# Gated attention and quantised MLP block on one core: means subtracted on GpSimd, MLP weights rounded on VectorE, and four pairs of roots taken together

## What is computed

```python
def _layernorm(x, axis=-1, eps=1e-05):
    return (x - mean(x)) / sqrt(var(x) + eps)

# xattn: q = layernorm(x), k = v = ctx
qp, kp = proj(q), proj(ctx)                  # two 128x128 linears, the same for both
attn   = softmax(qp @ kp.T * 128**-0.5 + mask)
x      = x + tanh(g_xattn) * (attn @ ctx)

# ffn on layernorm(x): fixed_quant(v, 8 bits, f) = clip(round(v * 2**f), -128, 127) / 2**f
h = relu(fixed_quant(fixed_quant(xn, 4) @ fixed_quant(w1, 6).T + fixed_quant(b1, 6), 4))
x = x + tanh(g_ffn) * (fixed_quant(h, 4) @ fixed_quant(w2, 6).T + fixed_quant(b2, 6))
```

## Time and profile before

| | |
|---|---|
| median of 3 runs | 66.66 us (66.5 to 66.83) |
| the profiled execution, its own time | 66.68 us |
| span of that execution, first to last instruction | 64.9 us |
| busy: TensorE, VectorE, ScalarE, GpSimd | 57.8, 54.7, 52.4, 44.5 us |
| granted TensorE clock, mean over the span | 1.0 of full speed |
| last VectorE instruction (the last `result`) | 62.23 to 62.71 us |

### The profile page before, as it was taken

How to read it: one execution, slowest core, us unless ns; L and a number is a source line. 1 busy time by engine, 2 the same in 40 slices (tenths; PEclk the granted TensorE clock), 3 DMA queues, 4 the chain that set the end, 5 groups by cost and what they waited for, 6 DMA issues and landing times.

```text
span 64.9 us, 1898 instructions
## 1 busy us (share of the span) xinstructions
PE 57.8 (89%) x565; PEld 45.9 (71%) x565; DVE 54.7 (84%) x308; ACT 52.4 (81%) x145; POOL 44.5 (69%) x92
## 2 busy tenths in 40 slices
PE   4999799768999899999999999999999899996830
PEld 4988574517877788795979899699696779464510
DVE  4569959496999899999799999999999998888620
ACT  2600889849999979999999999999999969769600
POOL 5958888994790894698999999906997949133000
PEclk9999999999999999999999999999999999999999
DMA  0899999999980000000000003120300403041232
GB/s 0 231 412 405 416 414 406 414 400 408 406 324 23 0 0 5 10 0 0 10 0 0 0 5 119 58 111 0 128 34 0 169 8 144 18 162 73 93 121 81
DMA packets 3324, 9.09 MB, mean 140 GB/s; under 512 B 369, under 2 KB 754, under 8 KB 3314
## 3 DMA queue, kind: packets, MB, share of 16 engines
q1 hardware_dynamic: 3312, 8.98, 35.9%
q10 hardware_dynamic: 2, 0.00, 0.0%
HBM read 6.88 MB, written 2.10 MB: 138 GB/s over the span
## 4 chain that ended last, share of the span: by engine, by line
POOL 38%; issue 14%; DMA 14%; ACT 10%; DVE 9%; PE 4%; SPq 4%; POOLq 1%; ACTq 1%; DVEq 0%
POOL xq L377 17%; DMA load_sb<-in_packed 14%; POOL rs L359 12%; ACT pr L597 4%; POOL xn L367 4%; SPq L326 4%; DVE st L641 3%; POOL rs L355 2%; ACT prT L606 2%; PE bank_A L483 2%; DVE load_sb L707 2%; PE bank_O L524 2%; ACT xn L573 1%; DVE mv L644 1%; ACTq L149 1%
## 5 line engine op out<-in xcount | busy, mean ns | idle before, releaser
L624 ACT ACTIVATE h<-bank_H,fb_q 128x512 int8<-128x512 f32 (+2 forms) x28 | 16.2, 645 | 2.2 <-PE bank_H L509 2.1
L641 DVE BATCH_NORM_STATS2 st<-load_sb 128x6 f32<-128x128 f32 x64 | 14.0, 279 | 2.4 <-DMA load_sb<-in_packed 2.3
L359 POOL TENSOR_TENSOR rs<-ve,half 128x4 f32<-128x4 f32 (+2 forms) x9 | 8.5, 941 | 9.3 <-DVE nm L648 9.3
L597 ACT ACTIVATE pr<-sc,mn 128x120 f32<-128x120 f32 x32 | 12.4, 408 | 0.9 <-DVE mn L695 0.9
L377 POOL TENSOR_SCALAR xq<-load_sb,nm,rs 128x128 int8<-128x128 f32 x28 | 12.3, 456 | 0.8 <-POOL rs L359 0.2
L355 POOL TENSOR_TENSOR rs<-ve,half 128x4 f32<-128x4 f32 (+2 forms) x9 | 8.5, 942 | 2.6 <-DVE nm L648 2.6
L367 POOL TENSOR_SCALAR xn<-load_sb,nm,rs 128x128 f32<-128x128 f32 x22 | 9.6, 448 | 0.5
L467 PEld LDWEIGHTS bank_S<-kpT,xaT 128*128 128x128 f32 x64 | 8.1, 191 | 2.6 <-issue 2.3
L483 PE MATMUL bank_A<-load_sb,prT 120*128 120x128 f32 x64 | 9.1, 283 | 0.3 <-ACT prT L606 0.3
L707 DVE SCALAR_TENSOR_TENSOR load_sb<-bank_A,rec,load_sb 128x128 f32<-128x128 f32 x32 | 9.1, 343 | 0.4 <-DVE rec L700 0.3
L524 PE MATMUL bank_O<-w_q,h 128*128 128x128 bf16 x128 | 9.2, 219 | 0.2
(11 more groups left out here) (80 smaller groups left out, 102.0 us busy)
## 6 DMA issues: line engine op xcount, KB each, us to landing
load_sb<-in_packed SPq DMA_DIRECT2D x6, 496.0 KB, 8.0
out_y<-y_sb SPq DMA_DIRECT2D x6, 256.0 KB, 2.0
load_sb<-in_packed SPq DMA_DIRECT2D x2, 512.0 KB, 11.0
load_sb<-in_packed SPq DMA_DIRECT2D x1, 576.0 KB, 14.2
load_sb<-in_packed SPq DMA_DIRECT2D x1, 514.0 KB, 6.1
load_sb<-in_packed SPq DMA_DIRECT2D x1, 448.0 KB, 5.3
load_sb<-in_packed SPq DMA_DIRECT2D x1, 432.0 KB, 12.7
load_sb<-in_packed SPq DMA_DIRECT2D x1, 428.0 KB, 13.3
```

What stands on the lines that cost most here:

```text
L359: nc.gpsimd.tensor_tensor(rs2[:, of(g, n=1)], ve2[:, of(g, n=1)], half[:, of(g, n=1)], ALU.pow).then_inc(rs2_done, 1)
L597: nc.scalar.activation(pr[i][:, j, :], sc[i][:, j, :], ACT.Exp, scale=-1.0, bias=mn[:, of(g, j, 1)], accum_out=den[:, of(g, j, 1)]).then_i ...
L624: nc.scalar.activation(low_byte(h16[g % RING], hcols(c, g)), bank_H[c][:, cols(g)], ACT.Relu, bias=fb1_q[:, c:c + 1]).then_inc(h_act[c], 1)
L641: nc.vector.bn_stats(st[:, START[g] + j, :], x_of(g, j)).then_inc(st_done, 1)
```

## The change

1. `layer_stats` no longer makes `nm`. `normalise_pool` and `quantise_pool` read the mean itself and subtract it; `scale_means` becomes one instruction on VectorE with two multiplications.
2. `scale_weights` moves from ScalarE to VectorE, as three `tensor_scalar` instructions.
3. Both norms write into one `ve` and one `rs` (`[P, 2 * B]`), laid out so that the second norm of group g and the first norm of group `JOINED[g]` are neighbours. For g = 1, 2, 3, 4 that is group 5, 6, 7, 8: `rstd2(g)` takes both with one instruction, and `rstd1` of groups 5 to 8 is gone.
4. All the tables are new: the order, and the shares. VectorE's tiles of `xn` go from 0,0,0,0,0,1,2,0,0 to 0,0,2,0,0,0,0,0,0; its tiles of `xq` from 2,1,0,0,0,0,0,0,1 to 2,1,1,0,0,1,0,0,1; its relu chunks from 0,0,1,1,2,1,1,1,1 to 0,2,1,1,0,2,1,2,2. `FILLERS` go from 70 products to 47. `LOADS`, `TILES` and the rings stay.

```diff
-SPANS = [0, 1, 2, 3, 4, 5, 6, 7, 8, 9]
+JOINED = [0, 5, 6, 7, 8, 0, 0, 0, 0]
...
-XN_ON_POOL = [1, 2, 3, 2, 4, 3, 2, 3, 2]
-XN_ON_ACT = [2, 2, 1, 2, 0, 0, 0, 0, 0]
-XQ_ON_POOL = [1, 3, 4, 4, 4, 4, 4, 3, 1]
-RELU_ON_ACT = [4, 4, 3, 3, 2, 3, 3, 3, 3]
+XN_ON_POOL = [2, 1, 2, 2, 4, 4, 4, 3, 2]
+XN_ON_ACT = [1, 3, 0, 2, 0, 0, 0, 0, 0]
+XQ_ON_POOL = [1, 3, 3, 4, 4, 3, 4, 3, 1]
+RELU_ON_ACT = [4, 2, 3, 3, 4, 2, 3, 2, 2]
...
-    row_maxima=[1244, 1470, 1921, 2513, 2868, 3151, 3630, 4255, 4573],
+    row_maxima=[1029, 1402, 1947, 2329, 2769, 3255, 3557, 4106, 4432],
...
             def rstd2(g):
-                pool.wait_ge(ve2_done, 2 * g + 2)
-                nc.gpsimd.tensor_tensor(rs2[:, of(g, n=1)], ve2[:, of(g, n=1)], half[:, of(g, n=1)],
-                                        ALU.pow).then_inc(rs2_done, 1)
+                pool.wait_ge(ve2_done, g + 1)
+                at = roots(2, g)
+                if JOINED[g]:
+                    pool.wait_ge(ve1_done, JOINED[g] + 1)
+                    at = slice(at.start, roots(1, JOINED[g]).stop)
+                nc.gpsimd.tensor_tensor(rs[:, at], ve[:, at], half[:, 0:at.stop - at.start], ALU.pow).then_inc(rs2_done, 1)
...
-                    nc.gpsimd.tensor_scalar(xn[g % RING][:, tile(j)], x_of(g, j), nm1[:, of(g, j, 1)],
-                                            rs1[:, of(g, j, 1)], ALU.add, ALU.mult).then_inc(xn_pool, 1)
+                    nc.gpsimd.tensor_scalar(xn[g % RING][:, tile(j)], x_of(g, j), mv1[:, START[g] + j, 0:1],
+                                            rs[:, roots(1, g, j)], ALU.subtract, ALU.mult).then_inc(xn_pool, 1)
...
-                nc.vector.tensor_scalar(ve[:, at], mv[:, at, 1], EPS, scale ** -2, ALU.add, ALU.mult).then_inc(ve_done, 1)
-                nc.vector.tensor_scalar(nm[:, at], mv[:, at, 0], -1.0, None, ALU.mult).then_inc(ve_done, 1)
+                nc.vector.tensor_scalar(ve[:, roots(norm, g)], mv[:, of(g, n=1), 1], EPS, scale ** -2, ALU.add, ALU.mult).then_inc(ve_done, 1)
...
-                nc.vector.tensor_tensor(nr1[:, of(g, n=1)], nm1[:, of(g, n=1)], rs1[:, of(g, n=1)],
-                                        ALU.mult).then_inc(nr1_done, 1)
+                nc.vector.scalar_tensor_tensor(out=nr1[:, of(g, n=1)], in0=mv1[:, of(g, n=1), 0], scalar=-1.0,
+                                               in1=rs[:, roots(1, g)], op0=ALU.mult, op1=ALU.mult).then_inc(nr1_done, 1)
...
+            def scale_weights():
+
+                wait_load(dve, "mlp")
+                nc.vector.tensor_scalar(mp_8[:, :], mp_sb[:, :], W_SCALE, None, ALU.mult).then_inc(quant8, 1)
+                dve.wait_ge(row_in, 16)
+                nc.vector.tensor_scalar(fb2_8[:, :], row_sb[:, 2:2 + D], W_SCALE, None, ALU.mult).then_inc(quant8, 1)
+                dve.wait_ge(quant8, 1)
+                nc.vector.tensor_scalar(w1_q[:, :], mp_8[:, 0:C * P], 1.0 / W_SCALE, None, ALU.mult).then_inc(w1_up, 1)
```

More of the change, by code:

```diff
@@ L109 @@
+    mlp_out=[2840, 3650, 4142, 4501, 4854, 5197, 5448, 5713, 5915],
+    result=[2997, 3841, 4296, 4770, 5032, 5337, 5617, 5844, 6023],
+    relu_dve2=[0, 3352, 0, 0, 0, 5125, 0, 5683, 5898],
+    relu_dve3=[0, 3646, 4038, 4364, 0, 5193, 5483, 5736, 5936],
+    keep_warm0=[385.5],
+    keep_warm1=[586.5],
+    keep_warm2=[643.5],
+    keep_warm3=[754.5],
+    keep_warm4=[996.5],
 )
-FILLERS = [8, 38, 19, 5]
+FILLERS = [9, 26, 2, 6, 4]
 class Share(list):
@@ L211, in flamingo_gated_block, with norm_of, roots @@
         zeros_h = sb("zeros_h", [P, P // 2], BF16)
-        half = sb("half", [P, B])
-        def norm(n):
-            return (sb(f"st{n}", [P, B, 6]), sb(f"mv{n}", [P, B, 2]), sb(f"ve{n}", [P, B]), sb(f"nm{n}", [P, B]),
-                    sb(f"rs{n}", [P, B]))
-        st1, mv1, ve1, nm1, rs1 = norm(1)
-        st2, mv2, ve2, nm2, rs2 = norm(2)
+        half = sb("half", [P, 2 * TG])
+        def norm_of(n):
+            return sb(f"st{n}", [P, B, 6]), sb(f"mv{n}", [P, B, 2])
+        st1, mv1 = norm_of(1)
+        st2, mv2 = norm_of(2)
+        ve, rs = sb("ve", [P, 2 * B]), sb("rs", [P, 2 * B])
+        roots_at, end = {}, 0
+        for g in range(G):
+            for norm, group in ((2, g), (1, JOINED[g] or None)):
+                if group is not None:
+                    roots_at[norm, group], end = end, end + TILES[group]
+        for g in range(G):
+            if g not in JOINED or g == 0:
+                roots_at[1, g], end = end, end + TILES[g]
+        def roots(norm, g, j=None):
+            if j is None:
+                return slice(roots_at[norm, g], roots_at[norm, g] + TILES[g])
+            return slice(roots_at[norm, g] + j, roots_at[norm, g] + j + 1)
         mn, den, rec = (sb(n, [P, B]) for n in ("mn", "den", "rec"))
@@ L277, in wait_chunk, with wait_rs1 @@
                 engine.wait_ge(h_dve[c], RELU_DVE[c].before(g + 1))
-        def span_of(g):
-            return sum(first <= g for first in SPANS[1:-1])
+        def wait_rs1(engine, g):
+            if g and g in JOINED:
+                engine.wait_ge(rs2_done, JOINED.index(g) + 1)
+            else:
+                engine.wait_ge(rs1_done, sum(not h or h not in JOINED for h in range(g + 1)))
         def wait_xn(engine, g):
@@ L376, in quantise_pool @@
                 for j in range(XQ_POOL[g]):
-                    nc.gpsimd.tensor_scalar(low_byte(xq16[g % RING], tile(j)), x_of(g, j), nm2[:, of(g, j, 1)],
-                                            rs2[:, of(g, j, 1)], ALU.add, ALU.mult).then_inc(xq_pool, 1)
+                    nc.gpsimd.tensor_scalar(low_byte(xq16[g % RING], tile(j)), x_of(g, j), mv2[:, START[g] + j, 0:1],
+                                            rs[:, roots(2, g, j)], ALU.subtract, ALU.mult).then_inc(xq_pool, 1)
             def widen_weights():
@@ L400, in split_base @@
                 pool.wait_ge(base_cp, 5)
-            schedule(once=dict(widen_weights=widen_weights, split_base=split_base), rstd1=(rstd1, [int(g in SPANS) for g in range(G)]), rstd2=rstd2,
+            schedule(once=dict(widen_weights=widen_weights, split_base=split_base), rstd1=(rstd1, [int(not g or g not in JOINED) for g in range(G)]), rstd2=rstd2,
                      normalise_pool=(normalise_pool, XN_POOL), quantise_pool=(quantise_pool, XQ_POOL))
```

128 lines of the change are left out of this document (55 added, 73 removed).

## The result

| | before | changed |
|---|---|---|
| median | 66.75 us (66.5 to 67.11, 4 runs) | 75.23 us (74.32 to 75.41, 4 runs) |
| ratio | | 1.124 [1.113, 1.134] |
| profiled execution, its span | 66.68, 64.9 us | 75.2, 73.4 us |

The forecast was 65.9 us, with a range of 65.0 to 66.9. The change costs 8.5 us. First the page of the changed kernel: busy time, tenths in 40 slices, and the chain that ended last, by engine and by line.

A forecast was written before the change was run, and what follows sets the result against it. VectorE and ScalarE were taken as full in the middle. On VectorE, 2.5 us more work (57.2) plus idle cut from 8.0 to 4.7 ends at 61.9 against 62.71, -0.8: 65.9 us, range 65.0 to 66.9.

The forecast's parts named there:

- Its subtraction reads as many operands as the addition: GpSimd's normalising tiles: subtracting the mean costs no more than adding `nm`; three tiles stay at 1.31 us.
- The price I named in case: GpSimd, if subtraction or the mean's stride cost a tenth: 0.04 us a tile, 50 tiles, 2 us added.
- The account: VectorE until its last `result` ends: work 54.7 to 57.2 us, idle 8.0 to 4.7, end 61.9 against 62.71.
- The weights: Three weight instructions moved to VectorE: 2.0 us by a relu's slope, low end 1.2.
- the middle's idle time: VectorE's idle time from 15.10 to 49.77 us: 1.2 us, left unchanged.
- rival 1: VectorE's middle idle empties too, or weights cost the low end: 64.8 to 65.3 us; chance 0.17.
- the sign that the reasons are wrong: VectorE's idle time does not fall by about 3 us, or its work does not rise by 2 to 3.
- The places: Expected trace marks: first exponential about 12 us, eight-column roots 1.65, `hidden` of group 5 near 52.1, last `result` ending 61.9.
- Rival 2, late roots: GpSimd's joined roots make group 1's `xq` late for TensorE: chain 4.8 us, time 67.1 to 67.6; chance 0.13.
- on the path they save nothing: Four joined roots save GpSimd 1.5 us of work but no time, since it has 8 us free mid-kernel.
- Rival 3, held-up GpSimd: GpSimd and VectorE hold each other up at weights and quantising: some 0.5 us of gain goes, 66.4; chance 0.13.
- 23 products of zeros fewer, all where it waits anyway: TensorE: dropping these products falls in waiting time; granted clock expected to stay at 1.0.

The follow-up runs named there:

- b_sub: Kernel before with one edit: GpSimd subtracts the mean in both norms instead of adding `nm`, which is still made; 75.12 us, ratio 1.126.
- a_add: Changed kernel with `nm` made on VectorE again and GpSimd adding it; four runs 65.10 to 65.82 us (ratio 0.978), one 68.50.
- a_fill: `a_add` with more products of zeros on TensorE (9, 38, 14, 14, 4); 66.01, 66.35, four of 67.7 to 67.8, and 69.62 us.
- a_add2: The same kernel as `a_add`, measured a second time; 68.15 to 68.65 us in all six runs, ratio 1.022.
- a_wact: `a_add` with the MLP weights scaled on ScalarE again, as three `activation` instructions; 68.63 to 68.95 us (four runs), 70.38 and 70.59.
- b_few: Kernel before with fewer products of zeros (8, 22, 2, 5 for 8, 38, 19, 5); 66.74 to 68.05 us in eleven runs.

## Why the prediction was wrong

- **The step that failed:** "Its subtraction reads as many operands as the addition, so I price that at nothing: 1.31 us for three tiles stays". Three tiles of `xn` or `xq` take 2.35. The count of operands was no reason: no row of the trace had a subtraction on this engine, so it was an unseen operation, to be bounded like the weights. The price I named in case, a tenth of a tile, came to 2 us; it was 0.35 us on each of 50 tiles, 17.5 us on an engine whose idle time I put at 8 in the middle. `b_sub` gives all of the loss (+8.4 us).
- *The rest of the sum.* The account counted `nm` as gone, 1.3 us; with it back the account says 67.2 us for `a_add` (my expectation for that run allowed only 0.8 and said 66.0 to 66.8). Measured were 65.1 to 65.8 and 68.2 to 68.7, so no level confirms it. Two terms were mis-sized. The weights took 1.1 to 1.2 us, not 2.0: by the step, 0.60 for the 1028 columns. That is the estimate that I had set beside my sum from the Trainium skill, "VectorE: DVE Perf Modes", section "The perf-mode tier table", and this trace agrees with the page, not with my slope from the relu, which reads PSUM. And the middle's idle time, which I left at 1.2 us, fell to 0.7 between 15.10 and 49.77 in `a_fill` (34.00 of 34.67 busy): part of rival 1, whose sign (under 0.5 between 15 and 49) is just missed at 0.63. In all VectorE works 57.2 us until its last `result` in `a_fill`, 2.5 more than before, and is idle for 5.2, 2.8 less. That is near the 2.5 and 3.3 of my account, but `nm`, 1.3 us, is in the work, so the agreement is partly luck. In the changed kernel itself the idle time rose, from 8.0 to 15.1 us (56.2 of 71.27 busy), which I had named as the sign that the reasons are wrong.
- *The places.* `a_fill` is the one run with the repaired shares and order that has a profile and a quick start. There `hidden` of group 5 is at 52.08 (I said 52.1), the roots of eight take 1.64 us (1.65), and TensorE does not wait for GpSimd's `xq` of group 1. The first exponential is at 12.96 (about 12), and the last `result` runs from 61.93 to 62.41 (to end at 61.9): 0.3 us of the 0.8 are won. The lower runs of `a_add` won more, but have no profile.
- *Rival 2, late roots.* The chain from group 1's roots to its last `xq` was to take 4.8 us; it takes 25.30 to 30.11 in `a_fill`, 4.8, and TensorE, which transposes this `xq` at 30.96, does not wait for it. In the changed kernel it takes 26.86 to 34.07, 7.2 us. What I gave as its sign (waits for `xq`, holes in ScalarE's and VectorE's rows between 28 and 40) did appear, for another cause: a sign that two causes share tells neither. The joins, "on the path they save nothing", saved 0.4 us.
- *Rival 3, held-up GpSimd.* Its sign appeared too, tiles well above 0.45 us, and again for the other cause: `b_sub` has 0.80 to 0.81 with VectorE's list as before. What there is of the rival is small. The four-column root that runs beside the weights takes 1.45 us in `a_add2` and 1.01 with the weights on ScalarE (`a_wact`): 0.4 us of what I had allowed, and none of the loss. It fits the rule I cited from the Trainium skill, "SBUF — State Buffer", section "Who interferes with whom".
- *TensorE.* "23 products of zeros fewer, all where it waits anyway" is not borne out. In the order of before, 33 fewer cost 0.8% and more (`b_few`). What the 23 alone cost in the new order no run isolates: putting them back and more (`a_fill`) brought no lower time. And the clock did not stay: it is 0.50 from 40 to 43 us in the changed kernel, after TensorE had waited for GpSimd, a cost that follows from the first.

No version here is surely better than before. `a_add` beats the kernel before by 1.2 us at its lower level and loses 1.5 at its upper one.

## What to carry over

An operation that no row shows on an engine has no price, however like its neighbour it looks: multiply your doubt by the count before you call it nothing (0.35 us by 50 is 17.5 us of work, and the whole result). Idle time of an engine does not absorb added work in full: set the work added against all waits of that engine for a floor of the loss (here 17.9 less 11.9, 6.0 us; 9.6 were absorbed and 8.3 lost), and do not count on the floor, since 8.0 us of added work cost 1.4 in one place and 9.8 cost 4.3 in another. An order that no longer waits for one thing may wait for the next: the loads before, TensorE's start after. And time a kernel several times before its median is believed: one whose first microseconds can go two ways has two medians.
